# Moving one conversion a tile earlier, and neighbour sums to other places of PE's queue, in a two-layer graph network

## The chip, the core and the metric

The kernel runs on one core of a Trainium2 chip. The metric is device time in microseconds (us), the median of three runs. PE is the matrix engine, PEld its weight loads, DVE the vector engine, ACT the scalar engine, POOL the general engine, SP the queue that starts DMA transfers. Each engine works through its own program in order; engines wait for one another through semaphores.

## The reference, cut to what matters

There are 3125 nodes with 128 features and 100000 edges (src, dst, one of 9 types). Two layers follow one another:

```python
msg = x[src] @ W_msg.T + b_msg + edge_embed[type]
messages = segment_sum(msg, dst)                  # sum over the edges into each node
x1 = layernorm(x + gru_cell(messages, x))         # "first pass": gates r, z, n
h = relu(x1 @ w_self1 + mean_agg(x1) @ w_neigh1 + b1)    # "second pass"
out = layernorm(x1 + h @ w_self2 + mean_agg(h) @ w_neigh2 + b2)   # "third pass"
```

## The kernel before

**Counting.** The kernel first builds the adjacency counts AT, one column per destination node, one row per source node, in 25 tiles of 128 destinations. For each batch of 6 x 128 edges DVE writes one-hot rows D (L618) and S (L624), and PE multiplies them (L923, `count_tile`). The S rows carry several counts packed into one number. ACT moves a finished tile out of PSUM (`packed_out`), PE turns it (`turn_tile`, L901), ACT copies it (`packedT_in`), DVE cuts it into digits (`take_digits`, L613), and ACT stores the digits as columns of AT (`store_digits`, L1310, L1313), some tiles later. Between the batches PE already sums neighbour features for groups 0 to 4 (`early_sum`, L880), a group being 512 destinations (4 tiles); there are six groups of 512 and a rest of 64, numbered 0 to 6, so the sixth group is group 5.

**Feature parts.** The sums must be exact, so x is split into three bf16 parts held in `xp`. ACT writes the high part at the start; DVE forms the rest in tile 1 (`x_rest`, L663); ACT writes the middle part from it (`x_mid`, L1347, seven pieces); DVE forms the low part in tile 2 (`x_low`, L669, which waits for `x_mid`). ACT's program for tile t is `tile_steps(t)`: from tile 1 on `packed_out(t - 1)`, from tile 2 on `packedT_in(t - 2)`, which waits for PE's turning of tile t - 2, placed after PE's first product of tile t. `x_mid` stands behind `tile_steps(2)`.

**Tail of counting.** After the last tile is turned, its digits are taken and stored, DVE sums all counts (`verdict`, L699), PE sums that over the partitions with one small product (L948), DVE turns it into a flag, and all engines read the flag (`is_general_after_flag`): it chooses between this path and a general path for inputs that break the packing. PE does nothing else there.

**First pass.** A loop over the seven groups q. PE: `fills[q][0]`, the messages of group q + 1 (L1017, L1019), the turning of type counts of group q + 2 (`turn_types`, L1007), `fills[q][1]`, the gate products of group q + 1 (L1030 to L1033), and the turning of the new rows of group q (`rows_back`, L1041). The fills are neighbour sums that nobody waits for at that moment: 25 tiles x 3 parts for group 5 and for the rest of 64 (`late_sum`, L1057, both into PSUM bank 1, one after the other), then the sums of x1 for groups 0 and 1 of the second pass (`p2_first`, L1094, bank 1, `p2_second`, L1105, bank 2). `p2_first` waits until both late sums have been copied out, all of these p2 sums wait for the x1 tiles they read (`p1_low`), and `p2_second` waits for the last type counts to have left bank 2 (`p1_c`). After the loop the rest of these sums follows, and `p2_close` (L1188) adds the last tile and begins the second pass.

ACT in the same loop: `gate_functions(q)` (sigmoid, sigmoid, tanh), at q = 0 and q = 3 `late_out` (copies a late sum out of bank 1 and waits for that sum to end), `types_out(q + 2)` (L1440), `stage_types(q + 3)`, and `normed(q - 1)`, whose square root (L1411) DVE's layernorm of group q - 1 needs. DVE: `new_input(q)`, `message_copy(q + 1)` (L733), `pass1_norm(q - 1)`, `residual_rows(q)`, whose last instruction (L755) ends `y` of group q. `rows_back(q)` on PE and `gate_functions(q + 1)` on ACT wait for that `y`.

Of the kernel before, what the change touches and what calls it, by code (L numbers as in the profile page):

```python
# [21 lines left out]
TILES = -(-N // P)  # L22
# [27 lines left out]
STORES = LANES + 1  # L50
# [5 lines left out]
NC = TILES // 4  # L56
PARTS = 3
# [4 lines left out]
EARLY_PLAN = (0,) * 7 + (3, 3, 5, 3, 5, 3, 5, 6, 5, 6, 6, 6, 8, 9, 10, 11, 18, 13)  # L62
EARLY_BEGIN = tuple(sum(EARLY_PLAN[:t]) for t in range(TILES + 1))
assert EARLY_BEGIN[TILES] <= EARLY * TILES
SCRATCH = 2048


def graph_kernel(nc, x, xT, dst_c, dst_t, src_c, src_t, typ_c, typ_t, wmsgT, bmsg, embed, wihT, whhT,
# [17 lines left out]
    def place(region, name, shape, dt):  # L86
        t = nc.alloc_sbuf_tensor_at(name, shape, dt, offset=region[0])
        region[0] += nbytes(shape, dt)
        return t
# [11 lines left out]
    AT = place([AT_at], "AT", [P, TILES, DW], bf16)  # L101
# [39 lines left out]
    xp = place([B_at], "xp", [P, TILES, PARTS, F], bf16)  # L141
# [70 lines left out]
    with ctx:  # L212
        PS = ctx.enter_context(nc.psum_tensor("PS", [P, 8, 512], fp32))
        sems = {}

        def sem(name):
            if name not in sems:
                sems[name] = ctx.enter_context(nc.semaphore(name))
            return sems[name]
# [22 lines left out]
        def by_twos(q, start, end):  # L242

            return q.with_bounds(min_val=start, max_val=end - 2 + (end - start) % 2)
# [8 lines left out]
        def is_general(eng):  # L253
            return eng.value_load(flag_i[0:1, 0:1], min_val=0, max_val=1)
# [44 lines left out]
        def sizes(q):  # L299
            return (512, P, 4) if q < NC else (LASTW, LASTW, 1)  # L300
# [3 lines left out]
        def is_general_after_flag(eng):  # L304
            eng.wait_ge(sem("flag_set"), 1)
            return is_general(eng)
# [555 lines left out]
        def _(pe):  # L862
            mm = nc.tensor.matmul
# [21 lines left out]
            def early_steps(n0, n1):  # L885
                for q in range(EARLY):
                    j0, j1 = max(n0, q * TILES) - q * TILES, min(n1, (q + 1) * TILES) - q * TILES
                    if j0 < j1:
                        early_sum(q, j0, j1)
# [5 lines left out]
            def turn_tile(t):  # L895

                pe.wait_ge(sem("packed_out"), t + 1)
                if not isinstance(t, int) or t > 0:
                    pe.wait_ge(sem("packedT_in"), t)
                for g in range(GROUPS + 1):  # L900
                    ins = nc.tensor.transpose(PS[:, 4, g * P:(g + 1) * P], packed[:, g * P:(g + 1) * P], ident[:, :])  # L901
                ins.then_inc(sem("turned"), 1)
# [41 lines left out]
                count_tile(t, t % 2)  # L944
            early_steps(EARLY_BEGIN[TILES], EARLY * TILES)
            turn_tile(TILES - 1)
            pe.wait_ge(sem("verdict_set"), 1)
            mm(PS[0:1, 0, 0:1], ones[:, 0:1], verdict[:, :], start=True, stop=True).then_inc(sem("verdict_sum"), 1)  # L948
            general = is_general_after_flag(pe)

            def general_sum(n, width):
# [50 lines left out]
            def turn_types(name, q, w):  # L1002

                pe.wait_ge(sem(f"{name}_types_staged"), q + 1)
                for n in range(-(-w // P)):
                    rows = min(P, w - n * P)
                    ins = nc.tensor.transpose(PS[0:NTYPE, 2, n * P:n * P + rows], c_stage[0:rows, n, :], ident[0:rows, 0:rows])  # L1007
                ins.then_inc(sem(f"{name}_typeT"), 1)


            def messages(q):
                w = sizes(q)[0]
                if q >= 5:
                    pe.wait_ge(sem("late_out"), 2)
                if q:
                    pe.wait_ge(sem("p1_m"), q)
                mm(PS[:, 3, 0:w], wmsg_s[:, :], s_at(q)[:, 0:w], start=True, stop=False)  # L1017
                pe.wait_ge(sem("p1_c"), q + 1)
                mm(PS[:, 3, 0:w], emb_b[:, :], slot[7][0:NTYPE, 0:w], start=False, stop=True).then_inc(sem("p1_m_sum"), 1)  # L1019
# [24 lines left out]
            def late_sum(q, j0, j1):  # L1044

                w = sizes(q)[0]
                if q == NC - 1 and j0 == 0:
                    pe.wait_ge(sem("late_out"), 1)
                with pe.If(general):
                    if j1 == TILES:  # L1050
                        pe.sem_inc(sem("late_agg"), 1)
                    else:
                        pe.nop()
                with pe.Else():
                    for j in range(j0, j1):
                        for s in range(PARTS):
                            ins = mm(PS[:, 1, 0:w], xp[:, j, s, :], AT[:, j, q * 512:q * 512 + w],  # L1057
                                     start=(j == 0 and s == 0), stop=(j == TILES - 1 and s == PARTS - 1))
                    if j1 == TILES:
                        ins.then_inc(sem("late_agg"), 1)  # L1060
                pe.nop()
# [24 lines left out]
            def p2_first(j0, j1):  # L1086
                pe.wait_ge(sem("late_out"), 2)
                pe.wait_ge(sem("p1_low"), -(-j1 // 4))
                with pe.If(general):
                    pe.nop()  # L1090
                with pe.Else():
                    for j in range(j0, j1):
                        for s in range(PARTS):
                            mm(PS[:, 1, :], x1p[:, j, s, :], AT[:, j, 0:512], start=(j == 0 and s == 0), stop=False)  # L1094
                pe.nop()

            def p2_second(j0, j1):
                pe.wait_ge(sem("p1_c"), NC + 1)
                pe.wait_ge(sem("p1_low"), -(-j1 // 4))
                with pe.If(general):  # L1100
                    pe.nop()
                with pe.Else():
                    for j in range(j0, j1):
                        for s in range(PARTS):
                            mm(PS[:, 2, :], x1p[:, j, s, :], AT[:, j, 512:1024], start=(j == 0 and s == 0), stop=False)  # L1105
                pe.nop()

            fills = {0: (lambda: late_sum(NC, 0, TILES), lambda: late_sum(NC - 1, 0, 4)),
                     1: (lambda: late_sum(NC - 1, 4, 9), lambda: late_sum(NC - 1, 9, 13)),
                     2: (lambda: late_sum(NC - 1, 13, 18), lambda: late_sum(NC - 1, 18, 22)),  # L1110
                     3: (lambda: late_sum(NC - 1, 22, TILES), lambda: p2_first(0, 4)),
                     4: (lambda: p2_first(4, 8), lambda: p2_first(8, 10)),
                     5: (lambda: p2_first(10, 12), lambda: p2_first(12, 15)),
                     6: (lambda: p2_first(15, 18), lambda: p2_first(18, 20))}
            pe.wait_ge(sem("matrices_in"), 16 * len(matrices))
            turn_types("p1", 0, 512)
            messages(0)
# [4 lines left out]
            for q in range(NC + 1):  # L1122
                fills[q][0]()
                if q < NC:
                    messages(q + 1)
                if q + 2 <= NC:
                    turn_types("p1", q + 2, sizes(q + 2)[0])
                fills[q][1]()
                if q < NC:
                    gates(q + 1)  # L1130
                if q == NC:
                    p2_second(0, 6)
                rows_back(q)
            p2_second(6, 20)
            p2_first(20, TILES - 1)
            p2_second(20, TILES - 1)


# [136 lines left out]
            with pe.Else():  # L1275
                for n in range(4):
                    for j in range(begun, TILES):
                        ins = mm(PS[:, n, 0:PARTS * F], AT[:, j, n * P:n * P + P], xp[:, j, :, :].rearrange("p s f -> p (s f)"),
                                 start=False, stop=(j == TILES - 1))
# [3 lines left out]
            with pe.Fori(2, NC, 2) as q:  # L1283
                q = by_twos(q, 2, NC)
# [6 lines left out]
        def _(act):  # L1291
# [65 lines left out]

            for t in range(LAG):
                tile_steps(t, (t - 1) % 2)
                if t == 2:  # L1360
                    for c in range(NC + 1):
                        x_mid(c)
            act.wait_ge(sem("x_split"), NC + 1)
            with act.Fori(LAG, WIDE_TILES, 2) as t:
                t = by_twos(t, LAG, WIDE_TILES)
# [76 lines left out]
            def late_out(n, q):  # L1442
                w = sizes(q)[0]
                act.wait_ge(sem("late_agg"), n)
                act.wait_ge(sem("iota_t_set"), TILES + 1)
                with act.If(general):
                    act.sem_inc(sem("late_out"), 1)
                with act.Else():
                    a.activation(s_at(q)[:, 0:w], PS[:, 1, 0:w], ACT.Copy).then_inc(sem("late_out"), 1)
# [28 lines left out]
            stage_types("p1", 2)  # L1478
            for q in range(NC + 1):
                gate_functions(q)  # L1480
                if q == 0:
                    late_out(1, NC)
                if q == 3:
                    late_out(2, NC - 1)
                if q + 2 <= NC:
                    types_out(q + 2)
                if q + 3 <= NC:
                    stage_types("p1", q + 3)
                if q:
                    normed(q - 1)  # L1490
# [81 lines left out]
```

## Time and profile before

| what | us |
|---|---|
| median of 3 runs (lowest, highest) | 734.29 (732.76, 736.21) |
| the profiled execution | 735.67 |
| its span, first to last instruction | 733.9 |

The profile is of one execution. Times in the rows are counted from the start of its span. A row of the timeline gives start, duration, engine, line, operation, tiles, count of merged instructions, and in brackets how long the engine stood idle before it and what ended that. Merged instructions overlap a little at their ends, so the step from one row's start to the next one's is the better measure of a duration.

### The profile page before, as it was taken

The numbers are of one execution on the slowest core, as the hardware profiler recorded it, in microseconds if no ns is written. First come the engines' busy times: TensorE is split into PE (matmuls) and PEld (weight loads), VectorE is DVE, ScalarE is ACT, GpSimd is POOL, SyncE is SP. The second block draws the span as 40 slices with busy tenths as digits, with TensorE's granted clock in tenths as the row PEclk, the third lists the DMA queues.
The fourth block names the chain that finished last, engine by engine and source line by source line (L and its number), as shares of the span: only waits on it lengthen the run. The fifth ranks groups of instructions, "written<-read, shape, count | busy, mean of one in ns | idle before, by whom it ended". The sixth has DMA issues, their size and how long they took to land.

```text
span 733.9 us, 14577 instructions
## 1 busy us (share of the span) xinstructions
PE 648.3 (88%) x3061; PEld 308.6 (42%) x3061; DVE 466.9 (64%) x1469; ACT 242.2 (33%) x486; POOL 165.0 (22%) x348
## 2 busy tenths in 40 slices
PE   1668889999999999898967999789999999999995
PEld 0222333443433444343323444334555546666663
DVE  6879999999999999999992366641010001144334
ACT  3034553442332255566763245531121122100000
POOL 2432233333223333343430012130111011100000
PEclk9969999999999999999996999989999999999998
DMA  5000000000000000000011011010111011212200
GB/s 161 1 1 0 1 1 0 1 1 1 1 0 1 1 1 1 0 1 1 1 35 51 15 36 51 17 46 15 44 43 43 1 43 41 82 44 61 62 25 16
DMA packets 29441, 17.38 MB, mean 24 GB/s; under 512 B 1841, under 2 KB 28223, under 8 KB 29400
## 3 DMA queue, kind: packets, MB, share of 16 engines
q1 hardware_dynamic: 29400, 16.82, 7.8%
q8 instruction: 28, 0.46, 0.3%
q14 instruction: 13, 0.11, 0.0%
HBM read 10.38 MB, written 6.44 MB: 23 GB/s over the span
## 4 chain that ended last, share of the span: by engine, by line
PE 59%; DVE 22%; issue 9%; DVEq 6%; ACT 2%; POOL 0%; ACTq 0%; POOLq 0%
DVE S L624 12%; PE PS L1267 11%; PE PS L923 11%; PE PS L996 9%; PE PS L880 5%; DVE D L618 4%; PE PS L1178 3%; PE PS L1057 3%; PE PS L1105 2%; DVEq L624 2%; PE PS L1231 2%; PE PS L1094 2%; PE PS L1166 2%; PE PS L1167 1%; PE PS L1030 1%
## 5 line engine op out<-in xcount | busy, mean ns | idle before, releaser
L624 DVE TENSOR_SCALAR S<-iota_h,src_col,src_w 128x440 bf16<-128x440 f16 x749 | 253.2, 399 | 0.2 <-issue 0.2
L923 PE MATMUL PS<-S,D 128*128 128x449 bf16 x780 | 213.1, 363 | 36.8 <-DVE S L624 32.9
L477 POOL COPY S<-T 128x27 bf16 (+1 forms) x262 | 107.6, 412 | 222.2 <-PE PS L923 210.0
L923 PEld LDWEIGHTS PS<-S,D 128*128 128x128 bf16 x780 | 75.3, 97 | 169.2 <-DVE S L624 127.7
L1310 ACT ACTIVATE AT<-digits 128x1152 uint8 (+5 forms) x75 | 77.2, 1031 | 148.6 <-DVE digits L613 148.6
L618 DVE TENSOR_TENSOR D<-iota_t,dst 128x384 bf16<-128x384 f16 x260 | 93.5, 360 | 13.9 <-PE PS L923 13.2
L880 PE MATMUL PS<-AT,xp 128*128 128x512 bf16 x375 | 100.6, 379 | 0.0
L1267 PE MATMUL PS<-xp,AT 128*128 128x384 bf16 (+1 forms) x525 | 85.6, 326 | 0.0
L996 PE MATMUL PS<-AT,x1p 128*128 (+2 forms) x375 | 68.8, 342 | 1.2 <-DVE slot L806 1.2
L1267 PEld LDWEIGHTS PS<-xp,AT 128*128 (+2 forms) x525 | 51.5, 98 | 33.9 <-issue 0.3
L923 PE MATMUL PS<-S,AT 128*128 128x449 bf16 x150 | 35.9, 378 | 19.2 <-DVE S L624 10.5
L880 PEld LDWEIGHTS PS<-AT,xp 128*128 128x128 bf16 x375 | 34.9, 97 | 31.2 <-issue 1.1
L996 PEld LDWEIGHTS PS<-AT,x1p 128*128 128x128 bf16 x375 | 31.6, 98 | 36.0 <-issue 2.1
L838 DVE TENSOR_REDUCE slot<-PS 128x512 f32<-128x1536 f32 (+1 forms) x7 | 11.1, 1585 | 53.0 <-PE PS L1267 46.0
L1340 ACT ACTIVATE S<-AT,src_w,src_wn 128x440 bf16 x37 | 27.9, 755 | 29.8 <-PE PS L923 29.3
L1411 ACT ACTIVATE sd<-meanvar,eps 128x4 f32<-128x4 f32 (+2 forms) x14 | 4.2, 298 | 99.6 <-DVE meanvar L773 99.6
L803 DVE COPY slot<-PS 128x512 f32<-128x512 f32 (+1 forms) x7 | 4.4, 625 | 50.7 <-PE PS L1159 50.7
L531 POOL TENSOR_TENSOR slot<-slot,xp 128x512 f32<-128x512 f32 (+1 forms) x7 | 7.4, 1051 | 118.2 <-ACT xp L1419 118.2
L923 PEld LDWEIGHTS PS<-S,AT 128*128 128x128 bf16 x150 | 13.3, 101 | 38.6 <-DVE AT L618 27.7
L531 POOL TENSOR_TENSOR slot<-slot,x1p 128x512 f32<-128x512 f32 (+1 forms) x7 | 9.1, 1300 | 90.1 <-ACT x1p L1419 90.1
L806 DVE TENSOR_TENSOR slot<-slot,PS 128x512 f32<-128x512 f32 (+1 forms) x7 | 4.3, 621 | 37.2 <-PE PS L996 37.1
L813 DVE TENSOR_TENSOR slot<-PS,b_b 128x512 f32<-128x512 f32 (+1 forms) x7 | 4.4, 633 | 36.2 <-ACT slot L1513 36.2
(167 smaller groups left out, 664.7 us busy)
## 6 DMA issues: line engine op xcount, KB each, us to landing
slot<-x_rows SPq DMA_DIRECT2D x12, 256.0 KB, 2.9
xstage<-x SPq DMA_DIRECT2D x6, 256.0 KB, 5.5
x_rows<-slot SPq DMA_DIRECT2D x6, 256.0 KB, 2.2
y_rows<-slot SPq DMA_DIRECT2D x6, 256.0 KB, 2.2
res_rows<-slot SPq DMA_DIRECT2D x6, 256.0 KB, 2.2
slot<-res_rows SPq DMA_DIRECT2D x6, 256.0 KB, 2.8
out_rows<-slot SPq DMA_DIRECT2D x6, 256.0 KB, 2.2
slot<-xT SPq DMA_DIRECT2D x3, 256.0 KB, 2.7
```

Source lines behind the costliest of these rows:

```text
L477: g.tensor_copy(S[:, where:where + V, SPAN:WIDE], T[:, :, ds(c0 + where, V)].rearrange("p k c -> p c k")).then_inc(sem("types_placed"), 1)
L531: g.tensor_tensor(rest, full, hi, ALU.subtract).then_inc(sem(f"{name}_rest"), 1)
L618: v.tensor_tensor(ring[:, half, :].rearrange("p u (a b) -> p u a b", b=2), iota_t[:, par, :].rearrange("p (a b) -> p a b", b=2).unsqueeze( ...
L624: v.tensor_scalar(S[:, u, 0:SPAN], iota_h[:, :], src_col[:, ds(c0 + u, 1)], src_w[:, ds(c0 + u, 1)], ALU.is_equal, ALU.mult).then_inc(sem( ...
L880: ins = mm(PS[:, EARLY_BANKS[q], :], xp[:, j, s, :], AT[:, j, q * 512:q * 512 + 512], start=(j == 0 and s == 0), stop=(j == TILES - 1 and ...
L923: mm(PS[:, par, 0:WIDE], ring[:, u, :], S[:, u, 0:WIDE], start=opens and u == 0, stop=last).then_inc(sem("tiles_summed" if last else "item ...
L996: ins = mm(PS[:, 0, 0:w], parts[:, j, s, :], AT[:, j, ds(q * 512, w)], start=(j == 0 and s == 0), stop=(j == TILES - 1 and s == PARTS - 1))
L1057: ins = mm(PS[:, 1, 0:w], xp[:, j, s, :], AT[:, j, q * 512:q * 512 + w], start=(j == 0 and s == 0), stop=(j == TILES - 1 and s == PARTS - 1))
L1178: ins = mm(PS[0:rows, bank, at:at + 2 * F], hid[a][:, n * P:n * P + rows], w2[:, a, :, :].rearrange("k w m -> k (w m)"), start=(a == 0), s ...
L1267: ins = mm(PS[0:rows, 4 * par + n, 0:PARTS * F], AT[:, j, ds(q * 512 + n * P, rows)], xp[:, j, :, :].rearrange("p s f -> p (s f)"), start= ...
L1310: a.activation(AT[:, 0:TILES - 1, ds(t * P, w)].rearrange("p (g f) m -> p f g m", f=DIGITS)[:, WORDS * lane:WORDS * lane + n, :, :], digit ...
L1340: a.activation(S[:, U - 1, 0:SPAN].rearrange("p (a n) -> p a n", a=8), near, ACT.Relu, scale=src_wn[:, ds(b.with_bounds(min_val=0, max_val ...
```

## The change

Three edits. First, ACT writes the middle part of x behind `tile_steps(1)` and no longer behind `tile_steps(2)`. Second, the sums of group 5 over tiles 0 to 8 (27 products) are issued by PE right after the last tile is turned: 18 ahead of the verdict's product and 9 behind it, with a wait for the stored digits of tiles 0 to 23. Third, the fills are dealt out anew: group 5 is now finished in the fills of q = 0 and 1, the rest of 64 is summed after it, in the second fill of q = 2; the first fills of q = 2 and 3 are empty; 48 products of `p2_second` move ahead of `rows_back(4)`, `rows_back(5)` and `rows_back(6)`, and some of `p2_first` behind the loop. On ACT `late_out` comes at q = 1 (group 5) and q = 2 (the rest), and no longer at q = 0 (the rest) and q = 3 (group 5).

```diff
+TAIL_STEPS = 9
@@
             turn_tile(TILES - 1)
+
+            def tail_sum(j0, j1):
+
+                pe.wait_ge(sem("digits_stored"), TILES * STORES)
+                for j in range(j0, j1):
+                    for s in range(PARTS):
+                        mm(PS[:, 1, :], xp[:, j, s, :], AT[:, j, (NC - 1) * 512:NC * 512], start=(j == 0 and s == 0), stop=False)
+
+            tail_sum(0, 6)
             pe.wait_ge(sem("verdict_set"), 1)
             mm(PS[0:1, 0, 0:1], ones[:, 0:1], verdict[:, :], start=True, stop=True).then_inc(sem("verdict_sum"), 1)
+            tail_sum(6, TAIL_STEPS)
             general = is_general_after_flag(pe)
@@
-                if q == NC - 1 and j0 == 0:
+                if q == NC:
                     pe.wait_ge(sem("late_out"), 1)
@@
-            fills = {0: (lambda: late_sum(NC, 0, TILES), lambda: late_sum(NC - 1, 0, 4)),
-                     1: (lambda: late_sum(NC - 1, 4, 9), lambda: late_sum(NC - 1, 9, 13)),
-                     2: (lambda: late_sum(NC - 1, 13, 18), lambda: late_sum(NC - 1, 18, 22)),
-                     3: (lambda: late_sum(NC - 1, 22, TILES), lambda: p2_first(0, 4)),
-                     4: (lambda: p2_first(4, 8), lambda: p2_first(8, 10)),
+            fills = {0: (lambda: late_sum(NC - 1, TAIL_STEPS, 13), lambda: late_sum(NC - 1, 13, 17)),
+                     1: (lambda: late_sum(NC - 1, 17, 21), lambda: late_sum(NC - 1, 21, TILES)),
+                     2: (lambda: None, lambda: late_sum(NC, 0, TILES)),
+                     3: (lambda: None, lambda: p2_first(0, 6)),
+                     4: (lambda: p2_first(6, 8), lambda: p2_first(8, 10)),
                      5: (lambda: p2_first(10, 12), lambda: p2_first(12, 15)),
-                     6: (lambda: p2_first(15, 18), lambda: p2_first(18, 20))}
+                     6: (lambda: p2_first(15, 16), lambda: p2_second(9, 16))}
@@
-                if q == NC:
-                    p2_second(0, 6)
+                if q == NC - 2:
+                    p2_second(0, 2)
+                if q == NC - 1:
+                    p2_second(2, 9)
                 rows_back(q)
-            p2_second(6, 20)
-            p2_first(20, TILES - 1)
+            p2_second(16, 20)
+            p2_first(16, TILES - 1)
             p2_second(20, TILES - 1)
@@
                 tile_steps(t, (t - 1) % 2)
-                if t == 2:
+                if t == 1:
                     for c in range(NC + 1):
                         x_mid(c)
@@
                 gate_functions(q)
-                if q == 0:
-                    late_out(1, NC)
-                if q == 3:
-                    late_out(2, NC - 1)
+                if q == 1:
+                    late_out(1, NC - 1)
+                if q == 2:
+                    late_out(2, NC)
```

## Rows read from the trace of the kernel before

**Rows 1.** DVE's timeline in tiles 2 and 3.

```profile
34.15 0.62 DVE L618 TENSOR_TENSOR AT<-iota_t,dst 128x384 bf16<-128x384 f16 x2
40.18 1.29 DVE L669 TENSOR_TENSOR xp<-xstage,xp 128x512 bf16<-128x512 f32 x2 [5.41 <-ACT xp L1347]
...
51.07 0.63 DVE L618 TENSOR_TENSOR AT<-iota_t,dst 128x384 bf16<-128x384 f16 x2
```

**Rows 2.** ACT's timeline up to the middle parts.

```profile
38.53 0.54 ACT L1297 ACTIVATE packed<-PS 128x440 f32<-128x440 f32 x1 [14.78 <-PE PS L901]
...
39.50 3.42 ACT L1347 ACTIVATE xp<-xstage 128x512 bf16<-128x512 f32 x7
```

**Rows 3.** PE's timeline at the start of tile 2.

```profile
35.15 2.43 PE L923 MATMUL PS<-S,AT 128*128 128x449 bf16 x6 [0.16 <-issue]
37.38 1.06 PE L901 MATMUL PS<-ident,packed 128*128 128x128 f32 x4
```

**Rows 4.** PE's timeline from the end of counting to the first fill.

```profile
382.88 0.66 PE L901 MATMUL PS<-ident,packed 128*128 128x128 f32 x4 [1.27 <-ACT Cn L1298]
387.73 0.19 PE L948 MATMUL PS<-verdict,ones 128*1 128x1 f32 x2 [4.20 <-DVE verdict L699]
390.13 1.01 PE L1007 MATMUL PS<-ident,c_stage 128*9 128x128 f32 x4 [2.21 <-ACT c_stage L1425]
...
392.79 2.07 PE L1019 MATMUL PS<-slot,emb_b 9*128 9x512 f32 x2
...
402.26 2.35 PE L1057 MATMUL PS<-AT,xp 128*128 128x64 bf16 x75
404.45 1.10 PE L1017 MATMUL PS<-sums,wmsg_s 128*128 128x512 f32 x2
```

**Rows 5.** PE's timeline in q = 1 of the first pass.

```profile
418.39 1.02 PE L1017 MATMUL PS<-sums,wmsg_s 128*128 128x512 f32 x2
419.34 1.12 PE L1019 MATMUL PS<-slot,emb_b 9*128 9x512 f32 x2
420.39 0.60 PE L1007 MATMUL PS<-ident,c_stage 128*9 128x128 f32 x4
420.83 2.75 PE L1057 MATMUL PS<-AT,xp 128*128 128x512 bf16 x12
423.43 1.02 PE L1030 MATMUL PS<-slot,wih_s 128*128 128x512 f32 x2
...
428.63 0.66 PE L1041 MATMUL PS<-ident,slot 128*128 128x128 f32 x4
429.13 3.40 PE L1057 MATMUL PS<-AT,xp 128*128 128x512 bf16 x15
```

**Rows 6.** PE's timeline late in the first pass and where the second begins.

```profile
468.28 0.66 PE L1041 MATMUL PS<-ident,slot 128*128 128x128 f32 x4 [1.00 <-DVE slot L755]
...
479.79 1.12 PE L1041 MATMUL PS<-ident,slot 128*128 128x128 f32 x4 [5.70 <-DVE slot L755]
...
503.90 0.81 PE L1188 MATMUL PS<-AT,x1p 128*128 128x512 bf16 x3
```

**Rows 7.** DVE's and ACT's timelines in the first pass.

```profile
421.04 0.59 ACT L1440 ACTIVATE slot<-PS 9x512 f32<-9x512 f32 x1 [3.11 <-PE PS L1007]
...
427.89 0.69 DVE L755 TENSOR_TENSOR slot<-slot,slot 128x512 f32<-128x512 f32 x1
...
446.85 0.58 ACT L1449 ACTIVATE sums<-PS 128x512 f32<-128x512 f32 x1
```

**Rows 8.** Windows: length, busy us of PE, PEld, DVE, ACT, POOL, PE's granted clock, DMA.

```profile
30.00:34.00 4.00, 1.29 (x4) 0.41 (x5) 4.00 (x12) 0.00 (x0) 1.32 (x2) 0.90 0.00 0
...
384.70:390.00 5.30, 0.19 (x2) 0.09 (x2) 2.18 (x8) 2.62 (x10) 0.00 (x0) 0.51 0.31 91
390.00:398.40 8.40, 8.27 (x17) 3.20 (x18) 2.28 (x8) 2.70 (x5) 0.00 (x0) 0.50 0.23 66
398.40:402.30 3.90, 3.90 (x12) 1.66 (x11) 0.00 (x0) 0.00 (x0) 0.00 (x0) 1.00 0.03 7
```

## The prediction

> **What bounds the kernel now.** I read DVE's timeline first, over counting, then PE's from the end of counting to the second pass, then what DVE and ACT do behind PE's idle times. In counting DVE is the busy engine, and its one long stop is in tile 2: it has written the rows of 34.15 and then does nothing until 40.18, 5.41 us, for ACT's middle parts [rows 1]. The rests that ACT needs for them are DVE's work of tile 1 and lie before 34.15, but ACT's program puts them behind the copy of tile 1's sums and of turned tile 0, and there it waited 14.78 us for PE's turning [rows 2]. From 382.88 on PE is what ends last. It is idle 4.20 us ahead of the verdict's product and 2.2 us behind it [rows 4], and the clock granted to it falls to its lower level (1.2 GHz) at about 384.7 and comes back at about 398.4, after PE had been busy 8.27 of 8.40 us [rows 8]. Then PE is busy nearly without a stop in the first pass, with 1.00 us of idle time at 468.28 and 5.70 us at 479.79, both for a new row of DVE's [rows 6]. From 503.90 on the change touches nothing. So three places can give time: tile 2, the tail with the slow start behind it, and the first pass.
>
> **Part 1, middle parts a tile sooner.** The seven pieces take 3.42 us on ACT [rows 2], which idles there in any case, and nothing else waits behind them: the next copy waits for PE's turning. DVE can go on at 34.77 and no longer at 40.18. From 40.18 to 51.07 DVE works 10.89 us without a stop [rows 1]. Moved ahead, that work meets PE: the first half of a batch may overwrite S only when PE has made the first three products of the pass that starts at 35.15, at 0.405 us each [rows 3], so at 36.4 and not at 36.06 (34.77 and the first two low parts, 1.29 [rows 1]); and the second batch must wait for PE's turning to 38.45 and three more products, to 39.7, where DVE is ready at about 38.8 (each half batch is about 1.17: 10.89 less seven low parts of some 0.6, in six halves). These two waits give back 0.4 + 0.9. Tile 3 then starts at 34.77 + 10.89 + 1.3 = 47.0 and not 51.07: **-4.0**. Everything in counting is placed by tile and not by time, so the shift is carried to the end. Bounds: -5.4 if PE runs at its upper level and the waits vanish; -3.0 if the loss to PE is repeated once in tile 3.
>
> **Part 2, 27 sums in the tail.** A sum costs 0.217 us (twelve from 420.83 to 423.43 [rows 5]). Eighteen take 3.9: from the end of the turning at 383.54 to 387.45, and the verdict's product started at 387.73 [rows 4]. The digits that they wait for are there by then: the turning itself waits for ACT's `packed_out` of the last tile (L1298 [rows 4]), and in ACT's program that store stands ahead of it. Nothing that another engine needs stands behind the new wait but the verdict. Nine more take 1.95, from 387.92 to 389.9, and the type turning started at 390.13. So the cover holds, by 0.2 to 0.3 us, at the upper clock level. Its price without that level is in the last rival. One thing no row shows: whether PE's sequencer can read the flag while nine sums still wait to run. If not, the reading, 1.8 to 2.2 us before [rows 4], starts at 389.9 and costs +1.6; I take 0, as PE shows no idle time where it passes a branch in the loop (the twelve sums of 420.83 start at the turning's heels [rows 5]), and keep +1.6 for the range. The Trainium skill ("TensorE: Matmul & The Clock Gate", "Architectural detail") gives TensorE a queue 64 deep; by it nine sums with their weight loads fit and the cost is 0.
>
> What the tail gives back at once is the clock. Kept busy, PE should not fall at 384.7. From 390.13 to the first fill at 402.26 it took 12.13 [rows 4]. At the upper level: type turning 0.44, messages 0.95 + 1.05 [rows 5], then DVE's copy of the message with its way there and back, 0.9, under which the next type turning fits, then gates 5.2 (423.43 to 428.63 [rows 5]): 8.5. **-3.6**. If the clock falls for a part of that stretch, half of that is lost: -1.8.
>
> **Part 3, the first pass.** I count from the first fill (402.26 before). There `rows_back` of q = 1 came at 26.4, of q = 4 at 66.0, of q = 5 at 77.5, and `p2_close` at 101.6 [rows 5, 6]. After the change:
> - q = 0 and 1 have 48 sums where there were 75 narrow ones (2.19 [rows 4]) and 39 wide ones: 10.4 against 10.65. Group 5 ends at 20.9, the gates behind it at 26.1.
> - Here is the added wait. ACT's `late_out` of q = 1 stands ahead of `types_out(3)` and the square root of group 0. Before, `types_out` began at 18.8 (421.04) and `y` of q = 1 came 7.54 later (428.58) [rows 7]. Now ACT waits for 20.9, copies (0.58, of which 0.5 ahead of the next [rows 7]), and `types_out` begins at 21.6: `y` at 29.15, where PE is ready at 26.1. PE idles 3.1 us.
> - q = 2: turning 0.5, messages 2.0, types 0.45, the 75 narrow sums 2.2, to 34.35; then `late_out` (64 columns, 0.2) and again 7.54: `y` at 42.1. PE, done with the gates at 39.5, idles 2.5.
> - q = 3: 0.5 + 2.0 + 0.45 + 18 sums 3.9 + gates 5.2: 54.2. q = 4: 0.5 + 18 sums 3.9 in three places + 2.0 + 0.16 + 5.2: 65.9. PE is the bound in both, and `p2_second`'s wait for `p1_c` is met: ACT's last `types_out` follows the tanh of q = 4, and PE has the gates of group 5 to do after that.
> - q = 5: bound by `y`, 11.5 after the one before (468.28 to 479.79 [rows 6]): 77.4. PE fills that time: 15 sums, the small products and 21 sums end at 76.3, so the idle time of 5.7 becomes 1.
> - q = 6: 0.5 + 24 sums 5.2, to 83.1, up to 1 us of waiting for the last `y`, then 48 sums 10.4: `p2_close` at 94.5 (93.5 to 94.7).
>
> So **-7.1**, if the clock stays up.
>
> **What takes some of it back.** Two new idle times, 3.1 and 2.5 us, stand between what PE bore at 468.28 (1.00 idle [rows 6], clock kept) and what made the clock fall: in 30 to 34 PE was idle 2.71 of 4.00 us, in pieces, and it fell [rows 8]. I expect one fall. If it comes in q = 1, the turning (0.5), messages (2.0) and types (0.45) take about 1.9 times as long (from 390.13 to 392.79, 2.66, the same turning and product that take 1.39 at the upper level [rows 4, 5]) and the narrow sums up to twice: 2.7 + 2.2 = 4.9, all ahead of `late_out` and so of `y`; 3.1 if the clock comes back under the narrow sums. In q = 2's idle time it costs about the same: 2.7 and part of the 18 sums behind. I take **+4.5**. The same skill page ("Why this matters for your kernels") warns of one long gap between bursts; rows 8 show a fall with four products between the gaps. By the page as it stands both idle times might pass, which is the second case below.
>
> Sum: -4.0 - 3.6 - 7.1 + 4.5 = -10.2. Against the profiled execution (735.67, span 733.9) that is 725.5; against the median 734.29 it is **724.1**.
>
> **The rivals.**
> - One fall, as summed: 724.1. Chance 0.45.
> - No fall: -14.7, 719.6. For it: both gaps are shorter than the 5.70 and 4.20 that are seen to cost the clock. Against it: rows 8, first line. 0.20.
> - Two falls, or one and a slow start (+1.8): -14.7 + 8, or + 6.3: 725.9 to 727.6. Against two: a fall in q = 1 delays PE by as much as `y`, so that less idle time is left in q = 2. 0.25.
> - ACT's wait is hidden after all (the sums end sooner than 20.9, or layernorm of group 0 has slack): 3 us off `y` and no idle time to lose the clock in: -14.7 - 3, 716.6. The root stands behind the copy in ACT's program, and the step of 7.54 is the root, the norm and the residual one after the other, so 0.05.
> - Slower: the clock falls before the tail sums have begun and stays down through q = 1. It had fallen at 384.7 with the turning behind it, so it could fall about then with the first sums just running. Then a sum costs 0.46 (0.405 for 449 columns [rows 3], times 512 / 449): 18 end at 391.8, the verdict and the flag of all five engines are 4 us late, nine more end at 396.1, the types start 6 late, the gain of 3.6 is gone, and both waits of ACT cost their 4.5. -4.0 + 6 - 7.1 + 9 = +3.9: 738. It decides from the point where the clock stays down beyond about 391. 0.03. That the early parts do nothing (DVE waits for PE as long as it did for ACT) would cost 4.0 in any case and turns no sign: 728. 0.02.
>
> **How the numbers follow.** A measurement can tell about 0.5%, 3.7 us. Faster than 730.6: all of the first, second and fourth case, and nearly all of the third and the last: 0.91. Same: 0.07. Slower: 0.02. The range runs from 718.5 (no fall, and the early parts at -5.1) to 729.5 (two falls and the flag's +1.6, rounded up): it leaves out the hidden wait below and the slow tail above.
>
> **What the profile after would show.** Right: DVE's idle time at the first low parts gone and tile 3 at about 47; PE busy to 387.5 less 4 and a granted clock of 1.00 through the first messages; ACT idle at the copy of group 5 for some 5 us in q = 1, ended by PE's sums; PE idle 3 us ahead of `rows_back(1)`, and a granted clock of 0.50 behind it; `rows_back(5)` with about 1 us of idle time. Wrong: no idle time ahead of `rows_back(1)` (then ACT's wait was hidden); the verdict's product over 0.3 us later, counted from the last turning (then the tail's cover was too thin); a clock of 1.00 all through the pass (then 719.6); from `p2_close` to the end other than the 230 us of before (then something is touched that I left out).

## The result and the profile after

| | before | after |
|---|---|---|
| median us (lowest, highest) | 735.25 (732.76, 736.45) | 725.07 (721.86, 726.86) |
| profiled execution: time, span | 735.67, 733.9 | 721.86, 720.1 |

The ratio is 0.9861, with a 95% interval of 0.9813 to 0.9909: 10.2 us less, where 10.2 were forecast. The two profiled executions lie further apart, 13.8 us: the profile after is of the fastest of the four, and why the others are longer is the first question of the experiments.

DVE's timeline at the start of tile 2 (columns as in [rows 1], brackets for idle time and what ended it):

```profile
34.16 0.61 DVE L619 TENSOR_TENSOR AT<-iota_t,dst 128x384 bf16<-128x384 f16 x2
34.69 1.27 DVE L670 TENSOR_TENSOR xp<-xstage,xp 128x512 bf16<-128x512 f32 x2
36.61 0.36 DVE L619 TENSOR_TENSOR D<-iota_t,dst 128x384 bf16<-128x384 f16 x1 [0.64 <-PE PS L924]
...
39.71 0.36 DVE L619 TENSOR_TENSOR D<-iota_t,dst 128x384 bf16<-128x384 f16 x1 [0.65 <-PE PS L924]
...
47.05 0.61 DVE L619 TENSOR_TENSOR AT<-iota_t,dst 128x384 bf16<-128x384 f16 x2
```

The low parts start at 34.69 and no longer at 40.18 [rows 1]. Two short waits for PE, 1.29 together, take the place of the 5.41, and tile 3 starts at 47.05 and not 51.07.

PE's timeline from the last turning of counting to the first fill, to be held against [rows 4]:

```profile
378.92 0.66 PE L902 MATMUL PS<-ident,packed 128*128 128x128 f32 x4 [1.27 <-ACT Cn L1311]
379.41 4.05 PE L954 MATMUL PS<-AT,xp 128*128 128x512 bf16 x18
383.76 0.19 PE L958 MATMUL PS<-verdict,ones 128*1 128x1 f32 x2 [0.30 <-DVE verdict L700]
383.89 2.12 PE L954 MATMUL PS<-AT,xp 128*128 128x512 bf16 x9
386.19 0.60 PE L1018 MATMUL PS<-ident,c_stage 128*9 128x128 f32 x4 [0.18 <-issue]
386.62 1.02 PE L1028 MATMUL PS<-slot,wmsg_s 128*128 128x512 f32 x2
...
394.73 2.75 PE L1068 MATMUL PS<-AT,xp 128*128 128x512 bf16 x12
```

The turning comes 3.96 earlier than before, which is the first edit. From it to the verdict's product are 4.84 us (4.85 before) and from there to the type turning 2.43 (2.40 before): the 27 sums cost the tail nothing. From the type turning to the first fill are 8.54 us and not 12.13.

PE's timeline in the first pass, and below it ACT's and one row of POOL's:

```profile
415.57 1.02 PE L1041 MATMUL PS<-slot,wih_s 128*128 128x512 f32 x2
...
424.02 0.66 PE L1052 MATMUL PS<-ident,slot 128*128 128x128 f32 x4 [3.13 <-DVE slot L756]
...
437.21 0.66 PE L1052 MATMUL PS<-ident,slot 128*128 128x128 f32 x4 [2.67 <-DVE slot L756]
...
472.20 0.66 PE L1052 MATMUL PS<-ident,slot 128*128 128x128 f32 x4 [1.09 <-DVE slot L756]
...
478.92 0.30 PE L1052 MATMUL PS<-ident,slot 128*64 128x128 f32 x1 [0.88 <-DVE slot L756]
...
482.28 5.36 PE L1105 MATMUL PS<-AT,x1p 128*128 128x512 bf16 x24
...
490.06 0.81 PE L1201 MATMUL PS<-AT,x1p 128*128 128x512 bf16 x3
```

```profile
415.94 0.60 ACT L1462 ACTIVATE sums<-PS 128x512 f32<-128x512 f32 x1 [5.22 <-PE PS L1068]
416.43 0.57 ACT L1453 ACTIVATE slot<-PS 9x512 f32<-9x512 f32 x1
...
429.51 0.22 ACT L1462 ACTIVATE sums<-PS 128x64 f32<-128x64 f32 x1 [1.17 <-PE PS L1068]
```

```profile
480.70 1.15 POOL L534 TENSOR_TENSOR x1p<-slot,x1p 128x512 bf16<-128x512 f32 x1 [0.74 <-ACT x1p L1434]
```

The idle time of 5.70 us ahead of the turning of q = 5 [rows 6] is down to 1.09. In its place stand two new ones, 3.13 and 2.67, ahead of the turnings of q = 1 and q = 2, and behind them is ACT, which waits 5.22 us at its copy of group 5 with the type counts and the root in its queue. `p2_close` comes at 490.06 and not 503.90, 13.84 earlier, and from there to the end are 230.0 us, as before.

The clock in those stretches (windows: length, busy us of PE, PEld, DVE, ACT, POOL, granted clock, DMA):

```profile
379.40:386.20 6.80, 6.31 (x32) 2.59 (x30) 3.58 (x12) 3.22 (x11) 0.00 (x0) 1.00 0.44 134
386.20:394.70 8.50, 8.36 (x25) 3.54 (x26) 2.09 (x7) 2.70 (x5) 0.00 (x0) 1.00 0.22 67
420.90:424.00 3.10, 0.00 (x0) 0.00 (x0) 2.99 (x4) 0.74 (x2) 1.90 (x2) 1.00 0.61 169
424.00:429.10 5.10, 5.08 (x86) 3.51 (x87) 2.84 (x7) 3.27 (x4) 0.97 (x1) 1.00 0.02 3
```

Where it was 0.50 for 14 us [rows 8] it is 1.00 now, and in this execution it is kept through the idle time of q = 1 as well, and through that of q = 2 (1.00 from 434.50 to 437.20): no fall, the second case of the prediction.

### The profile page after: what moved, and what is told of

It is laid out like the page before. It is cut to its first block, busy times and chain, and to the rows that moved or that the text cites. A ratio compares the mean times of both kernels' runs of the same rounds, so it can differ in the third digit from the quotient of the medians.

```text
span 720.1 us, 14577 instructions
## 1 busy us (share of the span) xinstructions
PE 642.2 (89%) x3061; PEld 306.6 (43%) x3061; DVE 466.7 (65%) x1469; ACT 242.3 (34%) x486; POOL 162.5 (23%) x348
## 4 chain that ended last, share of the span: by engine, by line
PE 55%; DVE 24%; issue 10%; DVEq 6%; ACT 3%; POOL 0%; DMA 0%; SPq 0%; ACTq 0%; POOLq 0%
DVE S L625 12%; PE PS L1280 11%; PE PS L924 11%; PE PS L1007 9%; PE PS L881 5%; DVE D L619 4%; PE PS L1191 3%; DVEq L625 2%; PE PS L1244 2%; PE PS L1068 2%; PE PS L1105 1%; PE PS L1179 1%; PE PS L1180 1%; DVEq L655 1%; DVE AT L619 1%
## 5 line engine op out<-in xcount | busy, mean ns | idle before, releaser
L478 POOL COPY S<-T 128x27 bf16 (+1 forms) x262 | 104.1, 398 | 220.4 <-PE PS L924 208.2
L619 DVE TENSOR_TENSOR D<-iota_t,dst 128x384 bf16<-128x384 f16 x260 | 91.6, 352 | 15.2 <-PE PS L924 14.5
```

Source lines behind the costliest of these rows:

```text
L478: g.tensor_copy(S[:, where:where + V, SPAN:WIDE], T[:, :, ds(c0 + where, V)].rearrange("p k c -> p c k")).then_inc(sem("types_placed"), 1)
L619: v.tensor_tensor(ring[:, half, :].rearrange("p u (a b) -> p u a b", b=2), iota_t[:, par, :].rearrange("p (a b) -> p a b", b=2).unsqueeze( ...
```

## The experiments

My theory was the prediction's: three gains of 4.0, 3.6 and about 7, a price that ACT's queue puts on the first pass, and a clock that may fall in the idle times so made. The rivals: the executions differ somewhere else; the start is faster because sums left the first pass and not because of the clock; ACT's copies have slack.

**The changed kernel again, twice, with a profile each.** No edit.

> The changed kernel itself, once more, on the same chip as the others of this group, with another profiled execution. My theory: the executions lie in groups, near 722 (mean granted clock 0.99), near 724 and near 726 to 727 (0.98), by whether and for how long the clock falls in PE's idle times of q = 1 and q = 2. If this profile is of an execution over 723, its windows show a granted clock of 0.50 from within one of the two idle times on, the idle time of 3.1 or 2.7 us is followed by messages of 3.8 us instead of 2.0, and p2_close comes later by just what the execution is longer. Rival: the longer executions lose their time in counting, ahead of the last turning.

> The changed kernel, a further profiled execution, so that at least one of the three shows the longer form. My theory: as for the run before it; with the clock kept 721 to 722.5, with one fall 723.5 to 727. Rival: long without a granted clock of 0.50 between the first fill and the fourth turning of rows.

Measured: 724.82 us median (723.24 to 726.20) in the first, beside 734.87 of before, ratio 0.9858 (0.9834 to 0.9882), and one execution of 726.05 in the second. The profiled executions took 725.1 and 726.05. They do not lie in groups, as was expected, and of all nine executions of this kernel on record only the one of the profile after is below 723. PE's timeline and windows of the second:

```profile
423.82 1.11 PE L1052 MATMUL PS<-ident,slot 128*128 128x128 f32 x4 [3.13 <-DVE slot L756]
424.72 1.92 PE L1028 MATMUL PS<-sums,wmsg_s 128*128 128x512 f32 x2
426.57 2.07 PE L1030 MATMUL PS<-slot,emb_b 9*128 9x512 f32 x2
428.57 1.02 PE L1018 MATMUL PS<-ident,c_stage 128*9 128x128 f32 x4
429.39 4.08 PE L1068 MATMUL PS<-AT,xp 128*128 128x64 bf16 x75
433.31 1.10 PE L1041 MATMUL PS<-slot,wih_s 128*128 128x512 f32 x2
...
441.37 0.66 PE L1052 MATMUL PS<-ident,slot 128*128 128x128 f32 x4 [2.67 <-DVE slot L756]
...
494.22 0.81 PE L1201 MATMUL PS<-AT,x1p 128*128 128x512 bf16 x3
```

```profile
420.70:423.80 3.10, 0.00 (x0) 0.00 (x0) 2.99 (x4) 0.74 (x2) 1.90 (x2) 0.86 0.60 169
423.80:430.00 6.20, 6.18 (x24) 2.89 (x25) 2.76 (x7) 3.27 (x4) 0.97 (x1) 0.50 0.01 3
430.00:432.00 2.00, 2.00 (x42) 2.00 (x40) 0.54 (x5) 0.00 (x0) 0.00 (x0) 0.50 0.00 0
432.00:434.00 2.00, 2.00 (x32) 1.76 (x30) 0.00 (x0) 0.32 (x2) 0.00 (x0) 0.70 0.00 0
```

The same idle time of 3.13 us, and here the clock falls within it. The messages take 3.85 us and the narrow sums 3.92, where they took 2.0 and 2.19 [rows 4, 5], and all of that lies ahead of ACT's second copy:

```profile
433.68 0.22 ACT L1462 ACTIVATE sums<-PS 128x64 f32<-128x64 f32 x1 [5.53 <-PE PS L1068]
```

That copy waits 5.53 us and not 1.17. The rows of q = 2 come 17.55 after those of q = 1 (13.19 in the profile after), 4.36 more; `p2_close` comes 4.16 later and the execution is 4.19 longer. In the first of the two profiles the clock falls a little later, at about 425.0, when PE has just begun again, and the price is 3.15 between the rows (16.34) and 3.24 of the execution. So both longer executions are longer by what this place costs, and the rival (counting) falls: their last turning stands at 378.83 and 378.72, beside 378.92.

**The idle times filled.**

```diff
+                if q in (1, 2):
+                    for n in range(12 if q == 1 else 10):
+                        mm(PS[:, 3, :], xp[:, 10 + n % 4, n % 3, :], AT[:, 10 + n % 4, 0:512], start=True, stop=True)
                 if q == NC - 2:
                     p2_second(0, 2)
```

> The changed kernel, with 12 and 10 additional products whose results are discarded in PE's idle times of q = 1 and q = 2 (bank 3, behind the gates, ahead of the turning of rows). ACT's wait is untouched. My theory: the changed kernel's runs from 721.9 to 726.9 differ by whether the clock falls in these two idle times; kept busy, it can't fall there, and all runs lie at 721 to 723.5, the mean granted clock of every run at 0.985 or above. Rival, the spread comes from another place (counting, the second pass): the same spread of 5 us as before, median 725, or later by the products.

Measured: 722.05 us, all five executions from 721.70 to 722.82, beside 735.97 of before, ratio 0.9810 (0.9788 to 0.9832). PE's timeline in q = 1 (one of the twelve products has no record):

```profile
421.69 2.75 PE L1144 MATMUL PS<-AT,xp 128*128 128x512 bf16 x11
424.99 0.66 PE L1052 MATMUL PS<-ident,slot 128*128 128x128 f32 x4 [0.55 <-DVE slot L756]
```

Work that nobody needs makes the kernel some 3 us faster at the median and closes the spread from 5.0 us, and 3.0 in the repetition, to 1.1. ACT's wait is as it was: the turning of q = 1 comes 37.83 behind the first type turning, as in the profile after, and `p2_close` 103.87, as there; only the clock is kept. That settles where most of the spread comes from. About 1 us of it is another place: this profile is of the longest of the five executions, 0.96 longer than the profile after, and its last turning of counting already stands 0.96 later (379.88). The kernel also gives the change without a fall: 13.9 us less than before.

**The first edit alone.** The kernel before with one line changed, ahead of `x_mid`.

```diff
-                if t == 2:
+                if t == 1:
```

> The kernel before with the first edit alone: ACT writes the middle parts behind tile 1's step. My theory: DVE's stop of 5.41 us goes, two short waits for PE come back, tile 3 starts at 47.0 instead of 51.07, and nothing downstream gives it back: 4.0 us less than before (3 to 5). Rival, the first edit only moves DVE's wait (DVE waits for PE as long as it did for ACT): 0 to 1 us less. In both, the granted clock still falls in the tail and comes back about 13 us later.

Measured: 731.97 us beside 735.97, ratio 0.9938 (0.9917 to 0.9959): 4.0 less. One of the six executions took 729.11; it has no profile, and why it is shorter stays open. Tile 3 starts at 47.06, and PE's tail is the old one, 4 us earlier:

```profile
383.68 0.19 PE L948 MATMUL PS<-verdict,ones 128*1 128x1 f32 x2 [4.19 <-DVE verdict L699]
386.08 1.01 PE L1007 MATMUL PS<-ident,c_stage 128*9 128x128 f32 x4 [2.21 <-ACT c_stage L1425]
...
398.55 2.35 PE L1057 MATMUL PS<-AT,xp 128*128 128x64 bf16 x75
```

The slow start is still there (12.47 from the type turning to the first fill), so the first edit and the clock are separate gains.

**Discarded products in the tail.** The kernel before with 18 and 9 products whose sums are overwritten; every real sum stays in the first pass.

```diff
...
+                for j in range(j0, j1):
+                    for s in range(PARTS):
+                        mm(PS[:, 1, :], xp[:, j, s, :], AT[:, j, (NC - 1) * 512:NC * 512], start=True, stop=True)
+
+            tail_sum(0, 6)
             pe.wait_ge(sem("verdict_set"), 1)
             mm(PS[0:1, 0, 0:1], ones[:, 0:1], verdict[:, :], start=True, stop=True).then_inc(sem("verdict_sum"), 1)
+            tail_sum(6, 9)
```

> The kernel before with 27 additional products in the tail of counting whose sums are discarded (bank 1 is overwritten later), 18 ahead of the verdict's product and 9 behind it; no real sum is moved, so the first pass has all its work. My theory: PE stays busy, the clock does not fall at 384.7, and the stretch from the first type turning to the first fill takes 8.5 us instead of 12.1: 3.6 us less than before. Rival, the gain at the start comes from moving the sums out of the first pass and not from the clock: 0 us, or slower by what the products delay the verdict and the flag (up to 1.6).

Measured: 732.85 us beside 735.97, ratio 0.9954 (0.9939 to 0.9969): 3.1 less. Its windows from the last turning to the first fill:

```profile
384.40:391.00 6.60, 6.12 (x29) 2.43 (x27) 3.38 (x12) 3.22 (x11) 0.00 (x0) 1.00 0.42 132
391.00:399.60 8.60, 8.40 (x25) 3.57 (x26) 2.17 (x7) 2.70 (x5) 0.00 (x0) 1.00 0.21 66
```

and PE's timeline at the type turning behind it:

```profile
391.06 0.60 PE L1017 MATMUL PS<-ident,c_stage 128*9 128x128 f32 x4 [0.18 <-issue]
```

The first fill starts at 399.61, 8.55 after that type turning, with no sum moved. So the faster start is the clock's doing. (In this profile the last turning stands at 383.79, 0.91 later than in the profile before; that time lies ahead of the added products.) The 27 real sums in that place also take 5.9 us (27 x 0.217) of PE's work out of the first pass; what they are worth there without the new deal of the fills was not run.

**ACT's copies behind the root.** The changed kernel, with both `late_out` calls moved behind `normed(q - 1)`.

```diff
-                if q == 1:
-                    late_out(1, NC - 1)
-                if q == 2:
-                    late_out(2, NC)
...
                 if q:
                     normed(q - 1)
+                if q == 1:
+                    late_out(1, NC - 1)
+                if q == 2:
+                    late_out(2, NC)
```

> The changed kernel, with ACT's two late copies behind the root and parts of the group before (normed) instead of ahead of the type counts. My theory: the idle times of 3.13 and 2.67 us ahead of the second and third turning of rows are the price of ACT's queue; with the copies behind, the type counts of q = 1 start about 3 us earlier, PE has no idle time there over 1 us, the clock has no place to fall in, and the runs lie together: 717 us, 3 to 4 below the profiled run of the changed kernel (721.86) and about 8 below its median, with a spread between runs under 3 us. Rival, DVE's own chain sets the rows and ACT's copy had slack: same as the changed kernel, 722 to 727, with the same spread.

Measured: 717.62 us (716.83 to 717.96) beside 735.97, ratio 0.9749 (0.9727 to 0.9771), 18.4 us less than before and the fastest of these kernels together with the last one below. ACT's timeline in q = 1 and PE's at the next turnings:

```profile
412.64 0.59 ACT L1453 ACTIVATE slot<-PS 9x512 f32<-9x512 f32 x1 [2.46 <-PE PS L1018]
...
419.48 0.58 ACT L1462 ACTIVATE sums<-PS 128x512 f32<-128x512 f32 x1
```

```profile
420.24 0.66 PE L1052 MATMUL PS<-ident,slot 128*128 128x128 f32 x4
...
432.05 0.66 PE L1052 MATMUL PS<-ident,slot 128*128 128x128 f32 x4 [1.29 <-DVE slot L756]
```

The type counts no longer wait for the sum, the copy runs in a gap of ACT's, and PE passes the turning of q = 1 without a stop; ahead of that of q = 2 it is idle for 1.29, a little more than the 1 us expected. The granted clock is 1.00 from 384 to 485 in this profile: the fall goes with the idle time. ACT's copies had no slack.

**Only the first copy behind.** As in the kernel above, but the copy of q = 2 stays ahead of the type counts.

```diff
-                if q == 1:
-                    late_out(1, NC - 1)
                 if q == 2:
                     late_out(2, NC)
...
                     normed(q - 1)
+                if q == 1:
+                    late_out(1, NC - 1)
```

> The changed kernel with ACT's copy of group 5 (q = 1) behind the root and ACT's copy of the rest (q = 2) left ahead of the type counts. My theory: each copy has its own price. Of the 4.4 us between the kernel with both copies behind (717.6) and the changed one whose idle times were filled (722.05), the first copy carries the larger part, about 3, since it waited 5.22 us on ACT and the second 1.17: 718.5 to 719.5, with at most one idle time over 2 us left, in q = 2, and so a smaller spread than the changed kernel. Rival: the second copy carries it, since the first is followed by a group that PE bounds anyway: 721 or more.

Measured: 719.58 us (718.76 to 720.40) beside 734.87, ratio 0.9786 (0.9765 to 0.9806). A little over what was expected: the profiled execution (720.27) shows the clock falling in the idle time of q = 2,

```profile
420.77 0.66 PE L1052 MATMUL PS<-ident,slot 128*128 128x128 f32 x4
...
433.97 1.11 PE L1052 MATMUL PS<-ident,slot 128*128 128x128 f32 x4 [2.68 <-DVE slot L756]
434.88 1.91 PE L1028 MATMUL PS<-sums,wmsg_s 128*128 128x512 f32 x2
```

and its four executions are two near 718.8 with a mean granted clock of 0.989 and two near 720.3 with 0.985. The medians of this group and of the one before it stand beside different times of the kernel before (734.87 and 735.97), so the price of each copy is read from the profiles. From the turning of q = 1 to that of q = 2 are 13.20 us here and 11.81 with both copies behind: the second copy costs 1.4. From the first type turning to the turning of q = 1 are 37.83 us in the profile after and 34.59 in both these kernels: the first copy costs 3.2. Together they are the 4.4 us between 717.62 and 722.05, to within 0.2.

**Six more sums into the idle times at the end of the loop.** Both copies behind; `p2_second` up to tile 10 in q = 5 and from 10 to 18 in q = 6.

```diff
-                     6: (lambda: p2_first(15, 16), lambda: p2_second(9, 16))}
+                     6: (lambda: p2_first(15, 16), lambda: p2_second(10, 18))}
...
-                    p2_second(2, 9)
+                    p2_second(2, 10)
...
-            p2_second(16, 20)
+            p2_second(18, 20)
```

> Both copies behind the root, and three sums moved into the idle time of 1.08 us ahead of the turning of q = 5 and six in all ahead of that of q = 6 (0.87 us idle). My theory: 6 sums of 0.217 leave the end of the loop, 1.3 us, and the turning of q = 6 is at most 0.3 later: 716.5, 1 us less than with the copies alone. Rival: the sums hold up the turnings, and the rows of q = 6 that end the first pass: 717.6 or more.

Measured: 717.43 us (717.03 to 717.62) beside 734.87, ratio 0.9759 (0.9743 to 0.9775), which is no different from 0.9749. PE's timeline from the turning of q = 5 on:

```profile
467.57 0.66 PE L1052 MATMUL PS<-ident,slot 128*128 128x128 f32 x4 [0.45 <-DVE slot L756]
...
474.77 1.47 PE L1116 MATMUL PS<-AT,x1p 128*128 128x512 bf16 x6 [0.18 <-issue]
477.64 5.35 PE L1105 MATMUL PS<-AT,x1p 128*128 128x512 bf16 x24 [1.40 <-POOL x1p L534]
```

The sums did leave the end, and a wait of 1.40 us for POOL's low part of group 5 took their place. My expectation missed it, and its rival did not name it: the turnings are not held up (that of q = 6 comes 88.12 behind the first type turning, and 88.10 with the copies alone). The 24 products at 477.64 begin with tile 16 but wait for the low parts up to tile 23, which are group 5's, and they start 10.07 behind the turning of q = 5. They do so in every profile with this order of sums, the profile after included (472.20 to 482.28, where POOL's row ends at 481.85): 10.07 or 10.08 each time. So what the first pass waits for last is the way of group 5's rows through ACT and POOL, and 36 sums stand behind it. That was so in the changed kernel already; there PE's own sums hid all but about 0.3 us of the wait.

## Why the prediction was right, point by point

- **Part 1, -4.0.** -4.0 alone and 4.02 in the trace. The two waits that were to give back 0.4 + 0.9 gave back 0.64 + 0.65.
- **Part 2, cover of the tail.** Held to 0.01 us at the verdict, and reading the flag did not wait for the nine sums: 2.43 against 2.40, so the +1.6 kept for the range was not needed. The queue of 64 that the Trainium skill states for TensorE ("TensorE: Matmul & The Clock Gate", "Architectural detail") agrees with that.
- **Part 2, the clock, -3.6.** 8.54 against a forecast of 8.5 in the trace, 3.1 by the median of the kernel that does this alone.
- **Part 3, ACT's wait.** Group 5 ended at 20.84 of the first fill (20.9), `rows_back` of q = 1 came at 29.29 (29.15), of q = 2 at 42.48 (42.1), of q = 5 at 77.47 (77.4); idle times of 3.13 and 2.67 were forecast as 3.1 and 2.5.
- **Part 3, the end.** Here the size was off: `p2_close` at 95.33 and not 94.5, -6.3 and not -7.1. That is also outside the 93.5 to 94.7 it gave. Its sum, 83.1 + 1 + 10.4, has the last `y` hold PE for a full 1 us, and it held PE for 0.88. What the sum leaves out is the turning of q = 6 itself with the 0.18 of idle time behind it, 0.48 together, and the wait of the 24 sums for group 5's low part, which puts them at 482.28 where PE's twelve sums before them would have put them at 482.0. It took PE's queue for what ends the first pass, and by the runs it is that wait: moving six sums away from there did not help.
- **The fall, +4.5.** Seen in two of the three profiles, 3.2 and 4.2 us, so 4.5 was too much. Where the clock was down from the turning to the end of the narrow sums, these took 3.92 and not twice 2.19, and the rows came 4.36 later and not 4.9; in the other execution it fell only behind the turning and was back shortly before the narrow sums ended, and the rows came 3.15 later. That this is near the 3.1 put down for a clock that comes back under the narrow sums is chance: they took 3.73. The one profile without a fall is the second case: -13.8 where -14.7 was forecast. Two falls in one execution were not seen in a profile. The warning of the Trainium skill ("TensorE: Matmul & The Clock Gate", "Why this matters for your kernels") against a long gap between bursts does not sort these cases by itself: the same 3.13 us kept the clock in one execution and lost it in two, and 2.68 us lost it in the kernel with the first copy behind.
- **The rivals.** That ACT's wait is hidden fell with the kernel that has the copies behind. The slow one needed a clock that stays down in the tail; it was at 1.00 there in all three profiles, and it was not tried what a lower one would cost.

So, but for the end of the first pass, the mechanisms are the ones forecast. That -10.2 was forecast and -10.2 measured is in part luck: the gain without a fall is 0.8 smaller than forecast and the fall is 0.3 to 1.3 cheaper, and the two errors offset each other. The median of four executions also depends on how many of them lost the clock; the time of one execution is 722 to 727, mostly by whether the clock falls in the idle time that the change itself made.

## What to carry to other kernels

When a copy out of PSUM is moved to where its sum has not ended, look at what stands behind it in the copying engine's program, and put it behind whatever the next group needs. An idle time of the matrix engine can cost, beside its length, what follows it at the lower clock (here 3.2 and 4.2 us behind 3.13), so a place to put sums is best chosen where the engine would otherwise stand still for some microseconds. When a sum waits for rows of its own pass, count the way of those rows as well as the engine's queue: here it set when the last 36 sums could start. When executions of one program differ, compare two profiled executions stretch by stretch before changing anything.

## What the runs showed of the hardware that I had not expected

An idle time of the same length, 3.13 us at the same place of the same program, lost the granted clock in two executions and kept it in one. The 2.67 or 2.68 us ahead of the turning of q = 2 kept it in all three, and lost it in the kernel with the first copy behind. In one execution it fell within the 3.13 us, and 9.4 us of uninterrupted PE work passed before it was back (423.82 to about 433.2). In the other it fell only at about 425.0, when PE had been busy again since 423.94, and was back at about 431.9; the messages with their product over 9 rows, the type turnings and the narrow sums were what PE did in that time. And with 22 discarded products, 4.8 us of PE time at the upper level, the kernel was 13.9 us below before at the median, and 10.2 and 10.1 without them.
